# Second cross attention of a two layer decoder: projections at every other step, keys stacked piece by piece through DRAM

## The chip, the cores and the metric

The kernel runs on one core of one Trainium2 chip. The metric is the device time of one launch in microseconds; lower is better.

## The reference, cut to what matters

The kernel computes a two layer decoder on 16 sequences of 56 tokens with 128 channels. Each layer is self attention, cross attention over 1500 context rows, and a mixture of experts. The change touches the cross attention of the second layer only, with 16 heads of 8 channels:

```python
def _L1_xattn_ref(q, k, v, W_q, b_q, W_k, b_k, W_v, b_v, W_o, b_o):   # k = v = ctx, (16, 1500, 128)
    qh = _split_heads(q @ W_q.T + b_q, bs)
    kh = _split_heads(k @ W_k.T + b_k, bs)
    vh = _split_heads(v @ W_v.T + b_v, bs)
    scores = jnp.einsum('bhqd,bhkd->bhqk', qh, kh) / jnp.sqrt(jnp.float32(D_K))
    weight = jax.nn.softmax(scores, axis=-1)
    attn = jnp.einsum('bhqk,bhkd->bhqd', weight, vh)
    concat = attn.transpose(0, 2, 1, 3).reshape(bs, -1, D_MODEL)
    return concat @ W_o.T + b_o
```

## The kernel before

Every engine has a program of its own, written out by hand, and they meet in semaphores. In this stage TensorE, ScalarE, VectorE and SyncE walk the same loop: `for g in range(NC * B + LAG)`, with `b, c = g // 12, g % 12`. One loop over b has 12 steps c = 0 to 11. Three batches are in work at once.

For batch b + 1, TensorE computes in each step two of the 24 "maxima" products (L1085, 500 columns each); VectorE takes the row maximum of each (L1410). Unit u has piece u % 3 of the keys (500 of 1500 columns), so step 0 reads pieces 0 and 1 and step 1 begins with piece 2. For the batch four steps behind (n = g - LAG) it computes the scores of one chunk of 125 keys (L1105), ScalarE takes the exponential (L1329), GpSimd adds up the chunks (L1234), and in odd steps TensorE multiplies two chunks with the values (L1119). The sums (L1127) and their reciprocal and scaling on VectorE (L1456, L1457) are at step 7, VectorE's first addition (L1433) at step 6.

For batch b + 2 (in the 14 loops b = 0 to 13) the context is projected. `keys` on TensorE (L1044) makes a piece of 128 x 500 in PSUM bank 7; ScalarE writes its high part to `late_kH` (L1295; the tile prob_b), VectorE the low part to `late_kL` (L1404; the tile ctx_area). `values` (L1050) makes four chunks of the values in the same bank, and ScalarE takes them out (L1302). In `project`, TensorE waits before each piece until the one before has left bank 7:

```python
elif piece < 4:
    pe.wait_ge(m["khi"], 3 * b + piece)
    pe.wait_ge(m["klo"], 3 * b + piece)
else:
    pe.wait_ge(m["vev"], 3 * b + piece - 3)
```

Keys are projected at steps 2, 3, 4 and values at steps 6, 8, 10.

The score products want each quad of heads (32 rows) as a stack of 96 rows, high, high, low, in `late_k[b % 3]` (the tile HL). `stack` on SyncE (L1277) waits for all three pieces and copies by DMA from SBUF to SBUF: for each of 4 quads three transfers of 32 rows x 1500 values. TensorE's first maxima of the batch wait for all twelve (`m["stack"]`). After it SyncE loads the context of the next batch (L1266). Before the loop, a run-in of 12 steps computes the maxima of batch 0 and projects batch 1; stack(1) is then wanted at the first step of the loop.

Of the kernel before, what the change touches and what calls it, by code (L numbers as in the profile page):

```python
# [23 lines left out]
B, S, D = 16, 56, 128  # L24
# [9 lines left out]
S2 = 1500  # L34
KC = 125
NC = S2 // KC
KB = 500
# [18 lines left out]
ADDS = NC - 2  # L56
Q_BANKS, V_BANKS = (7, 3, 4, 5), (6, 7, 3)
# [14 lines left out]
def decoder_kernel(nc, t, out):  # L72
# [4 lines left out]
    with ctx:  # L77
# [159 lines left out]
        inv_kept = [nc.dram_tensor(f"inv_kept{g}", (128, SIZES[g]), fp32).ap() for g in range(2)]  # L237
        x_kept = nc.dram_tensor("x_kept", (128, NTOK), fp32).ap()
# [48 lines left out]
        names = ("wqrep qp qhi qlo q0set qset ones kmm khi klo stack vmm vev mxmm mx nmsplit nmtr nmcopy nmlow nmrow "  # L287
# [749 lines left out]
        def late_tensor(pe):  # L1037
# [32 lines left out]
            def maxima(b, u):  # L1070

                s, w = u // NKB, u % NKB
                if u == 0:
                    pe.wait_ge(m["stack"], 16 * 12 * (b + 1))
                    if b:
                        pe.wait_ge(m["qset"], b)
# [80 lines left out]
            def rest():  # L1157
# [30 lines left out]
                for g in range(NC * B + LAG):  # L1188
# [8 lines left out]
                    if b + 2 < B and c in (2, 3, 4):  # L1197
                        project(b + 2, c - 2)
                    if b + 2 < B and c in (6, 8, 10):
                        project(b + 2, c // 2)  # L1200
# [59 lines left out]
        def late_sync(sp):  # L1260
# [8 lines left out]
            def stack(b):  # L1269

                sp.wait_ge(m["khi"], 3 * (b + 1))
                sp.wait_ge(m["klo"], 3 * (b + 1))
                if b >= 3:
                    sp.wait_ge(m["sc"], 2 * NC * (b - 2))
                for j in range(4):
                    for r, half in enumerate((late_kH, late_kH, late_kL)):
                        sp.dma_start(late_k[b % 3][r * QUAD:(r + 1) * QUAD, j * S2:(j + 1) * S2].bitcast(fp32),  # L1277
                                     half[j * QUAD:(j + 1) * QUAD, :].bitcast(fp32)).then_inc(m["stack"], 16)
# [9 lines left out]
        def late_scalar(act):  # L1288
            m = la

            def keys(b, piece, bank):
                act.wait_ge(m["kmm"], 3 * b + piece + 1)
                if b and piece == 0:
                    act.wait_ge(m["stack"], 16 * 12 * b)
# [62 lines left out]
            def rest():  # L1357
# [18 lines left out]
                for g in range(NC * B + LAG):  # L1376
# [5 lines left out]
                    if b + 2 < B and c in (2, 3, 4):  # L1382
                        keys(b + 2, c - 2, 7)
                    if b + 2 < B and c in (6, 8, 10):
                        values(b + 2, c // 2 - 3, 7)
# [10 lines left out]
        def late_vector(dve, chain):  # L1396
            m = la

            def keys(b, piece, bank):
                dve.wait_ge(m["khi"], 3 * b + piece + 1)  # L1400
                if b and piece == 0:
                    dve.wait_ge(m["stack"], 16 * 12 * b)
# [61 lines left out]
            def rest():  # L1464
# [16 lines left out]
                for g in range(NC * B + LAG):  # L1481
# [9 lines left out]
                    if b + 2 < B and c in (2, 3, 4):  # L1491
                        keys(b + 2, c - 2, 7)
# [736 lines left out]
```

## Time and profile before

| | |
|---|---|
| median of 3 runs | 1412.35 us (1408.24 to 1413.59) |
| the profiled execution, its own time | 1414.38 us |
| its span | 1412.6 us |
| PE busy | 95% of the span |
| the loop described above | from 894 us to 1306 us |
| mean granted TensorE clock | 0.979 |

Busy shares are averages over unlike stages. A matmul's end is modelled, so that a row of two matmuls is longer than the time until the next one may start; what a step takes is read from start to start. "idle before <-releaser" gives the time the engine stood still and what released it. SPq is the queue of SyncE: its rows are the issuing of DMAs, not their data.

### The profile page before, as it was taken

What the parts mean: (1) busy time and instruction counts of PE and PEld (TensorE: products, weight loads), DVE (VectorE), ACT (ScalarE), POOL (GpSimd) and SP (SyncE); (2) the same over time, 40 slices, a digit from 0 to 9 for tenths busy, and PEclk for the clock granted to TensorE, in tenths of its full rate; (3) what the DMA queues carried; (4) which work ended last, traced back from release to release, by engine and by line L of the source; (5) the groups of instructions that cost most, each with busy time, mean ns of one, the idle gap of its engine ahead of it and who ended that gap; (6) DMA issues with size and microseconds to landing.
All of it is one profiled execution on the core that took longest, in us unless ns stands there. A gap on an engine that the chain in (4) does not pass through costs nothing.

```text
span 1412.6 us, 25408 instructions
## 1 busy us (share of the span) xinstructions
PE 1337.2 (95%) x9220; PEld 1037.2 (73%) x9220; DVE 1051.9 (74%) x2127; ACT 863.9 (61%) x1849; POOL 735.0 (52%) x416
## 2 busy tenths in 40 slices
PE   7889999999999999999998987899999999999998
PEld 4548888888888888888875854566666666665687
DVE  6558778888778777888854577777778778785787
ACT  4537667666666666676632554466666666665675
POOL 5136443334444444433151374187887887884463
PEclk9999999999999999999998899899999999998999
DMA  3132222211122222221150130644645536440131
GB/s 86 60 94 52 57 58 58 53 39 41 47 56 58 52 57 58 57 58 28 44 160 2 59 77 25 142 119 103 140 111 120 144 88 147 97 96 2 59 109 42
DMA packets 71803, 104.39 MB, mean 74 GB/s; under 512 B 14670, under 2 KB 54934, under 8 KB 71550
## 3 DMA queue, kind: packets, MB, share of 16 engines
q1 hardware_dynamic: 60062, 91.39, 25.9%
q10 hardware_dynamic: 11616, 11.38, 2.9%
q8 instruction: 73, 1.20, 0.4%
q14 instruction: 52, 0.43, 0.1%
HBM read 63.65 MB, written 2.11 MB: 47 GB/s over the span
## 4 chain that ended last, share of the span: by engine, by line
PE 81%; DVE 9%; DMA 3%; ACT 3%; SPq 2%; issue 1%; ACTq 0%; POOL 0%; DVEq 0%; POOLq 0%
PE PS L702 10%; PE PS L716 6%; PE PS L690 5%; PE PS L1105 5%; PE PS L1085 5%; PE PS L1119 5%; PE PS L691 5%; PE PS L692 5%; PE PS L718 5%; PE PS L717 5%; PE PS L1044 3%; SPq L1277 2%; PE PS L1792 2%; PE PS L745 2%; PE PS L1794 2%; PE PS L1793 2%
## 5 line engine op out<-in xcount | busy, mean ns | idle before, releaser
L1234 POOL TENSOR_TENSOR QO_area<-QO_area,prob_a 125x896 f32<-125x896 f32 x150 | 315.2, 2101 | 100.2 <-DVE QO_area L1433 80.3
L868 ACT ACTIVATE HL<-PS 125x512 fp32r<-125x512 f32 (+1 forms) x384 | 206.6, 539 | 178.1 <-PE PS L702 161.3
L960 DVE TENSOR_TENSOR HL<-PS,HL 125x512 fp32r<-125x512 f32 (+1 forms) x384 | 238.1, 622 | 74.5 <-ACT HL L868 53.4
L1410 DVE TENSOR_REDUCE QO_area<-PS 112x1 f32<-112x500 f32 x384 | 237.4, 670 | 44.3 <-PE PS L1085 44.1
L1329 ACT ACTIVATE prob_a<-PS 125x448 f32<-125x448 f32 x384 | 187.6, 540 | 122.6 <-PE PS L1105 117.3
L775 POOL TENSOR_TENSOR HL<-ctx_area,ones 125x512 fp32r<-125x512 f32 (+1 forms) x64 | 93.0, 1453 | 245.4 <-PE PS L718 191.5
L1085 PE MATMUL PS<-HL 96*112 96x500 f32 x384 | 157.8, 480 | 16.9 <-DVE QO_area L1410 12.1
L716 PE MATMUL PS<-HL 125*128 125x512 f32 (+1 forms) x384 | 155.7, 405 | 2.2 <-DVE HL L960 1.7
L690 PE MATMUL PS<-HL 128*128 128x500 f32 x336 | 152.8, 455 | 4.3 <-DVE HL L930 3.9
L878 ACT ACTIVATE prob_a<-prob_a,neg_max 128x500 f32<-128x500 f32 x192 | 135.5, 707 | 25.3 <-DVE neg_max L952 24.0
L718 PE MATMUL PS<-HL 125*128 125x512 f32 (+1 forms) x384 | 140.4, 366 | 0.0
L717 PE MATMUL PS<-HL 125*128 125x512 f32 (+1 forms) x384 | 140.1, 365 | 0.0
L1105 PEld LDWEIGHTS PS<-HL 98*125 98x125 f32 x768 | 118.6, 190 | 27.8 <-ACT prob_a L1329 7.8
L1105 PE MATMUL PS<-HL 98*125 98x256 f32 x768 | 133.1, 293 | 2.8 <-ACT prob_a L1329 2.8
L691 PE MATMUL PS<-HL 128*128 128x500 f32 x336 | 130.9, 389 | 0.0
L692 PE MATMUL PS<-HL 128*128 128x500 f32 x336 | 130.6, 389 | 0.0
L702 PEld LDWEIGHTS PS<-ident,prob_a 128*125 128x125 f32 x768 | 113.4, 186 | 17.3 <-ACT prob_a L878 0.8
L1085 PEld LDWEIGHTS PS<-HL 96*112 96x112 f32 x384 | 60.8, 179 | 82.2 <-DVE QO_area L1410 56.7
L778 POOL TENSOR_TENSOR HL<-ctx_area,HL 125x512 fp32r<-125x512 f32 (+1 forms) x64 | 116.6, 1822 | 5.0
L702 PE MATMUL PS<-ident,prob_a 128*125 128x128 f32 x768 | 115.3, 272 | 0.4 <-ACT prob_a L878 0.4
L878 ACT ACTIVATE prob_b<-prob_b,neg_max 128x500 f32<-128x500 f32 x144 | 101.8, 707 | 0.0
L775 POOL TENSOR_TENSOR HL<-QO_area,ones 128x896 fp32r<-128x896 f32 x15 | 25.2, 1680 | 142.6 <-PE PS L692 129.0
(260 smaller groups left out, 2727.0 us busy)
## 6 DMA issues: line engine op xcount, KB each, us to landing
HL<-prob_b SPq DMA_DIRECT2D x128, 187.5 KB, 3.9
ctx_area<-in_ctx_T SPq DMA_DIRECT2D x16, 750.0 KB, 13.1
ctx_area<-in_ctx SPq DMA_DIRECT2D x16, 750.0 KB
HL<-ctx_area SPq DMA_DIRECT2D x64, 187.5 KB, 3.8
inv_area<-in_ctx_T SPq DMA_DIRECT2D x8, 750.0 KB, 4.1
prob_a<-in_ctx_T SPq DMA_DIRECT2D x8, 750.0 KB, 4.4
inv_area<-inv_kept ACTq DMA_DIRECT2D x16, 256.0 KB, 3.4
ctx_area<-in_L_ffn_W SPq DMA_DIRECT2D x16, 256.0 KB, 3.2
```

Source lines behind the costliest of these rows:

```text
L690: nc.tensor.matmul(dst, qH[b % 2][:, rows], kH[b % 2][:, cols], start=True, stop=False)
L702: mm = nc.tensor.transpose(PS[0:KC, 2 + k % 3, j * 128:(j + 1) * 128], tile_prob(GA * g + j)[:, k * KC:(k + 1) * KC], ident[:, :])
L716: nc.tensor.matmul(dst, v_hi, p_hi, start=k == 0, stop=False)
L717: nc.tensor.matmul(dst, v_lo, p_hi, start=False, stop=False)
L718: nc.tensor.matmul(dst, v_hi, p_lo, start=False, stop=k == NC - 1).then_inc(m["pv"], 1)
L868: nc.scalar.activation(pH[k % 3][0:KC, 0:width(g)], PS[0:KC, 2 + k % 3, 0:width(g)], ACT.Copy)\
L878: nc.scalar.activation(p, p, ACT.Exp, bias=neg_max[:, s:s + 1], accum_out=part_sum[:, s, j:j + 1]).then_inc(m["exp"], 1)
L960: nc.vector.tensor_tensor(pL[k % 3][0:KC, 0:width(g)], PS[0:KC, 2 + k % 3, 0:width(g)], pH[k % 3][0:KC, 0:width(g)].bitcast(fp32), ALU.sub ...
L1085: nc.tensor.matmul(PS[0:2 * S, w, 0:KB], late_q[b % 3][0:3 * QUAD, s * 2 * S:(s + 1) * 2 * S], late_k[b % 3][0:3 * QUAD, at:at + KB], star ...
L1105: mm = nc.tensor.matmul(PS[0:KC, 3 + half, a * SCOLS:(a + 1) * SCOLS], late_k[b % 3][:, j * S2 + c * KC:j * S2 + (c + 1) * KC], late_q[b % ...
L1234: nc.gpsimd.tensor_tensor(acc, acc, late_p[n % LATE_P], ALU.add).then_inc(m["padd"], 1)
L1410: nc.vector.tensor_reduce(late_part[b % 2][:, u // NKB, u % NKB:u % NKB + 1], PS[0:2 * S, u % NKB, 0:KB], AX, ALU.max).then_inc(m["mx"], 1)
```

## The change

The projections move to steps 2, 4, 6 (keys) and 8, 10, 11 (values). VectorE takes the low part of a key piece one step later (steps 3, 5, 7). `stack` works piece by piece: when a piece is ready, two transfers write its high and low part (128 x 500 each) to a DRAM scratch `keys_kept`, SyncE waits for both, and three transfers read it back, each to 32 rows and all four quads. There is a semaphore for each piece, and TensorE's first three maxima units each wait for their own.

```diff
--- before.py
+++ after.py
@@ -54,6 +54,7 @@
 LATE_P = 5
 SUM_STEP = (3, 7)
 ADDS = NC - 2
+PROJECTED = (2, 4, 6, 8, 10, 11)
 Q_BANKS, V_BANKS = (7, 3, 4, 5), (6, 7, 3)
 LAG = 4
 SCOLS = 256
@@ -235,6 +236,7 @@
         slot_kept = nc.dram_tensor("slot_kept", (E * B, S), fp32).ap()
         gates_kept = [nc.dram_tensor(f"gates_kept{l}", (E * B, S), fp32).ap() for l in range(2)]
         inv_kept = [nc.dram_tensor(f"inv_kept{g}", (128, SIZES[g]), fp32).ap() for g in range(2)]
+        keys_kept = [[nc.dram_tensor(f"keys_kept{i}{h}", (128, S2), fp32).ap() for h in range(2)] for i in range(2)]
         x_kept = nc.dram_tensor("x_kept", (128, NTOK), fp32).ap()
         vo_kept = nc.dram_tensor("vo_kept", (128, NH * 128), fp32).ap()
         vo_first = [x.rearrange("p (h c) -> p h c", h=NH // 2) for x in free[0:2]]
@@ -284,7 +286,7 @@
         ld_k = [sem("ld_k0")]
         ld_late = [sem(f"ld_late{i}") for i in range(2)]
 
-        names = ("wqrep qp qhi qlo q0set qset ones kmm khi klo stack vmm vev mxmm mx nmsplit nmtr nmcopy nmlow nmrow "
+        names = ("wqrep qp qhi qlo q0set qset ones kmm khi klo split stack0 stack1 stack2 vmm vev mxmm mx nmsplit nmtr nmcopy nmlow nmrow "
                  "sc exp pv first padd sum norm wo out").split()
         la = {n: sem(f"late_{n}") for n in names}
         ld_v = sem("ld_v")
@@ -1070,10 +1072,10 @@
             def maxima(b, u):
 
                 s, w = u // NKB, u % NKB
-                if u == 0:
-                    pe.wait_ge(m["stack"], 16 * 12 * (b + 1))
-                    if b:
-                        pe.wait_ge(m["qset"], b)
+                if u < NKB:
+                    pe.wait_ge(m[f"stack{w}"], 16 * 3 * (b + 1))
+                if u == 0 and b:
+                    pe.wait_ge(m["qset"], b)
                 if b == 0:
                     if u < NKB:
                         pe.wait_ge(m["qlo"], u + 1)
@@ -1194,10 +1196,8 @@
                     if 0 <= n:
                         scores(n // NC, n % NC, 0)
                         scores(n // NC, n % NC, 1)
-                    if b + 2 < B and c in (2, 3, 4):
-                        project(b + 2, c - 2)
-                    if b + 2 < B and c in (6, 8, 10):
-                        project(b + 2, c // 2)
+                    if b + 2 < B and c in PROJECTED:
+                        project(b + 2, PROJECTED.index(c))
                     if c == 0 and 0 <= b < B:
                         turn_maxima(b)
                     if n % 2:
@@ -1268,14 +1268,22 @@
 
             def stack(b):
 
-                sp.wait_ge(m["khi"], 3 * (b + 1))
-                sp.wait_ge(m["klo"], 3 * (b + 1))
-                if b >= 3:
-                    sp.wait_ge(m["sc"], 2 * NC * (b - 2))
-                for j in range(4):
-                    for r, half in enumerate((late_kH, late_kH, late_kL)):
-                        sp.dma_start(late_k[b % 3][r * QUAD:(r + 1) * QUAD, j * S2:(j + 1) * S2].bitcast(fp32),
-                                     half[j * QUAD:(j + 1) * QUAD, :].bitcast(fp32)).then_inc(m["stack"], 16)
+                for w in range(NKB):
+                    sp.wait_ge(m["khi"], 3 * b + w + 1)
+                    sp.wait_ge(m["klo"], 3 * b + w + 1)
+                    if b >= 3 and w == 0:
+                        sp.wait_ge(m["sc"], 2 * NC * (b - 2))
+                    if b >= 2:
+                        sp.wait_ge(m[f"stack{w}"], 16 * 3 * (b - 1))
+                    c = slice(w * KB, (w + 1) * KB)
+                    for h, half in enumerate((late_kH, late_kL)):
+                        sp.dma_start(keys_kept[b % 2][h][:, c], half[:, c].bitcast(fp32)).then_inc(m["split"], 16)
+                    sp.wait_ge(m["split"], 16 * 2 * (NKB * b + w + 1))
+                    for r, h in enumerate((0, 0, 1)):
+                        dst = late_k[b % 3][r * QUAD:(r + 1) * QUAD, :].rearrange("p (j n) -> p j n", j=4)
+                        sp.dma_start(dst[:, :, c].bitcast(fp32),
+                                     keys_kept[b % 2][h][:, c].rearrange("(j p) n -> p j n", j=4))\
+                            .then_inc(m[f"stack{w}"], 16)
 
             load(0)
             sp.wait_ge(x_ready, 3)
@@ -1290,8 +1298,8 @@
 
             def keys(b, piece, bank):
                 act.wait_ge(m["kmm"], 3 * b + piece + 1)
-                if b and piece == 0:
-                    act.wait_ge(m["stack"], 16 * 12 * b)
+                if b:
+                    act.wait_ge(m[f"stack{piece}"], 16 * 3 * b)
                 nc.scalar.activation(late_kH[:, piece * KB:(piece + 1) * KB], PS[:, bank, 0:KB], ACT.Identity,
                                      bias=xa_bias[:, 1:2]).then_inc(m["khi"], 1)
 
@@ -1379,10 +1387,10 @@
                     if 0 <= n:
                         exps(n // NC, n % NC, 0)
                         exps(n // NC, n % NC, 1)
-                    if b + 2 < B and c in (2, 3, 4):
-                        keys(b + 2, c - 2, 7)
-                    if b + 2 < B and c in (6, 8, 10):
-                        values(b + 2, c // 2 - 3, 7)
+                    if b + 2 < B and c in PROJECTED[0:3]:
+                        keys(b + 2, PROJECTED.index(c), 7)
+                    if b + 2 < B and c in PROJECTED[3:6]:
+                        values(b + 2, PROJECTED.index(c) - 3, 7)
                     if b + 2 < B and c == 5:
                         queries(b + 2)
                     if c == 0 and 0 <= b < B:
@@ -1398,8 +1406,8 @@
 
             def keys(b, piece, bank):
                 dve.wait_ge(m["khi"], 3 * b + piece + 1)
-                if b and piece == 0:
-                    dve.wait_ge(m["stack"], 16 * 12 * b)
+                if b:
+                    dve.wait_ge(m[f"stack{piece}"], 16 * 3 * b)
                 c = slice(piece * KB, (piece + 1) * KB)
                 nc.vector.scalar_tensor_tensor(late_kL[:, c], PS[:, bank, 0:KB], xa_bias[:, 1:2],
                                                late_kH[:, c].bitcast(fp32), ALU.add, ALU.subtract)\
@@ -1488,8 +1496,8 @@
                         maxima(b + 1, 2 * c + 1)
                     if c == 1 and 0 <= b < B:
                         low_maxima(b)
-                    if b + 2 < B and c in (2, 3, 4):
-                        keys(b + 2, c - 2, 7)
+                    if b + 2 < B and c - 1 in PROJECTED[0:3]:
+                        keys(b + 2, PROJECTED.index(c - 1), 7)
                     if n >= 0 and n % NC == 2:
                         first_add(n // NC)
                     if n > NC * (B - 1) + 1:
@@ -1878,7 +1886,8 @@
                     .then_inc(ld_w[par], 16)
 
             sp.wait_ge(la["vmm"], 3 * B)
-            sp.wait_ge(la["stack"], 16 * 12 * B)
+            for w in range(NKB):
+                sp.wait_ge(la[f"stack{w}"], 16 * 3 * B)
             for e in range(E):
                 load(e, e % 2)
```

## Rows read from the trace of the kernel before

**Rows 1.** One loop; columns: stretch, busy times, PE clock, DMA share, GB/s.

```profile
core 0: us, PE busy (x) PEld busy (x) DVE busy (x) ACT busy (x) POOL busy (x), PEclk, DMA share, GB/s
...
1035.00:1062.00 27.00, 25.82 (x216) 17.87 (x215) 20.67 (x34) 18.49 (x38) 22.51 (x12) 1.00 0.48 116
```

**Rows 2.** Waits between 930 and 1250 us: us in total, times, longest.

```profile
PE PS L1044 <- DVE ctx_area L1404: 8.5, 12, 0.7
...
PEld PS L1085 <- DMA HL<-ctx_area: 6.1, 12, 1.6
```

**Rows 3.** Timeline from step 10 of a loop to step 4 of the next.

```profile
1046.56 0.71 PE L1085 MATMUL PS<-HL 96*112 96x500 f32 x2
...
1047.58 1.04 PE L1050 MATMUL PS<-proj_w,prob_a 128*125 128x128 f32 x8
...
1048.38 0.70 PE L1085 MATMUL PS<-HL 96*112 96x500 f32 x2
...
1050.37 0.71 PE L1085 MATMUL PS<-HL 96*112 96x500 f32 x2
...
1051.42 0.69 PE L1085 MATMUL PS<-HL 96*112 96x500 f32 x2
...
1053.71 0.73 PE L1085 MATMUL PS<-HL 96*112 96x500 f32 x2
...
1055.20 1.02 PE L1085 MATMUL PS<-HL 96*112 96x500 f32 x2
...
1056.51 0.74 DVE L1404 SCALAR_TENSOR_TENSOR ctx_area<-PS,xa_bias,prob_b 128x500 fp32r<-128x500 f32 x1 [1.02 <-ACT prob_b L1295]
...
1057.39 1.08 PE L1044 MATMUL PS<-inv_area,proj_w 128*128 128x500 f32 x2 [0.70 <-DVE ctx_area L1404]
...
1059.30 0.71 PE L1085 MATMUL PS<-HL 96*112 96x500 f32 x2
```

**Rows 4.** SyncE's queue in one loop.

```profile
1037.49 1.14 SPq L1277 DMA_DIRECT2D HL<-prob_b  x2
...
1062.88 1.14 SPq L1277 DMA_DIRECT2D HL<-prob_b  x2
```

**Rows 5.** Columns as in rows 1: the stack, then a write to DRAM.

```profile
1039.00:1047.00 8.00, 7.51 (x77) 5.58 (x76) 7.23 (x11) 5.05 (x11) 5.80 (x3) 1.00 0.99 215
67.10:69.80 2.70, 2.70 (x6) 1.39 (x5) 0.00 (x0) 0.88 (x4) 0.00 (x0) 0.65 0.97 388
```

**Rows 6.** SyncE's queue around that write (two transfers, 1.05 MB).

```profile
66.27 0.82 SPq L643 DMA_DIRECT2D vo_kept<-ctx_area  x2
70.21 0.33 SPq L815 DMA_DIRECT2D ctx_area<-in_ctx_T  x1
```

**Rows 7.** TensorE around the DMA wait at the start of loop 1.

```profile
918.44 0.96 PE L1119 MATMUL PS<-prob_a,QO_area 125*32 125x224 f32 x16
921.09 0.71 PE L1085 MATMUL PS<-HL 96*112 96x500 f32 x2 [1.68 <-DMA HL<-ctx_area]
```

**Rows 8.** Columns as in rows 1: after the DMA waits at 894 and 921.

```profile
898.00:902.00 4.00, 3.20 (x5) 1.12 (x4) 2.33 (x4) 0.68 (x1) 0.00 (x0) 0.50 0.00 1
...
922.00:924.00 2.00, 2.00 (x14) 1.63 (x16) 2.00 (x5) 1.11 (x4) 1.86 (x2) 0.58 0.12 49
924.00:926.00 2.00, 2.00 (x19) 0.89 (x19) 0.21 (x2) 0.97 (x2) 1.86 (x2) 0.57 0.02 4
```

**Rows 9.** SyncE's queue: where the stacks of loops 0 and 1 begin.

```profile
907.60 1.14 SPq L1277 DMA_DIRECT2D HL<-prob_b  x2
...
934.78 1.14 SPq L1277 DMA_DIRECT2D HL<-prob_b  x2
```

**Rows 10.** Run-in: VectorE's first low part, TensorE's first steps of loop 0.

```profile
876.93 0.74 DVE L1404 SCALAR_TENSOR_TENSOR ctx_area<-PS,xa_bias,prob_b 128x500 fp32r<-128x500 f32 x1
...
894.24 0.68 PE L1085 MATMUL PS<-HL 96*112 96x500 f32 x2 [1.44 <-DMA HL<-ctx_area]
...
894.78 0.55 PE L1085 MATMUL PS<-HL 96*112 96x500 f32 x1
```

## The prediction

> **What bounds the kernel now.** I read the busy times first. In this stage TensorE is busy for 25.8 of 27 us, VectorE for 20.7 and GpSimd for 22.5, at full clock, with the DMA engines half used [rows 1]. So TensorE is nearest to a bound, but a row of two matmuls overlaps what follows, and its busy share does not say that it never stands. The reader should next take the waits: bank 7 makes it stand for a key piece's eviction (8.5 us over 12 loops), and the stack's DMA for 6.1 us over 12 loops, once for each loop [rows 2]. Then the timeline, from first maxima matmul to first maxima matmul (1000 us left off here): step 10, with a values projection, takes 46.56 to 48.38 = 1.82 us, step 11 (with two chunks of products) in 48.38 to 50.37 = 1.99, step 0 in 1.05, step 1 (products) in 2.29, step 2 (keys) in 1.49, but step 3, with keys and products, takes 55.20 to 59.30 = 4.10. In it the second key matmul starts at 57.39, after VectorE's low part (56.51 plus 0.74) has ended [rows 3]. Last, SyncE's queue: the stack begins 25.39 us after the one before it, which is the length of a loop, and its twelve transfers, started at 37.49, let TensorE go on at 50.37, 12.88 us later [rows 3, 4]. From there to the next stack are 12.51 us. Those two terms are the whole loop, so the loop is closed by a chain through the DMA: keys, stack, maxima, keys. It is this chain, more than TensorE's work, that the change rearranges.
>
> **Step 3 and step 11.** The number of matmuls, evictions and reductions stays the same. Steps 2 and 3 together are 5.59 us now. After the change step 2 keeps one projection (1.82, as step 10) and step 3 has products alone (2.0, as step 11): 3.82 together, 1.77 less. Steps 4 and 6 keep a projection each, and steps 8 and 10 too. Step 11 gains one: from 47.58 to 48.38 [rows 3], 0.80 us. Waits at the new places: the second key piece, at step 4, wants the low part made in step 3; step 3's reductions and low part end 0.45 + 1.25 + 0.74 = 2.44 us after step 3 begins, which is 0.44 into step 4, and the projection there comes 1.0 us into the step, as in step 10 (47.58). No wait. The piece at step 11 wants the eviction of step 10, with a step between. No wait. A loop would be 25.39 - 1.77 + 0.80 = 24.4 us by TensorE, 14 loops 13.6 us less.
>
> **VectorE.** Two low parts move into steps 5 and 7, where its first addition, the reciprocal and the scaling already crowd it. It loses the waits for ScalarE in steps 3 and 4 and so comes to step 5 earlier, by about the 1.5 us that it waits there now; 2 x 0.74 = 1.48 us more work [rows 3] lies there. I count 0; without that cover it is 1.5 us for each loop.
>
> **The stack.** This is the large term. L is the time from the first low part (in step 3, no longer step 4) until piece 2 has landed. TensorE reads pieces 0 and 1 in step 0 and piece 2 first in step 1. How much L is allowed? From step 4 to step 0 are 59.30 to 50.37 + 25.39 = 75.76, 16.46 us; plus 0.80 in step 11 and 1.05 for step 0 make 18.3; the low part ends 0.44 into step 4, so 17.9 us. From step 1 back to the low part are 2.29 + 1.82 + 2.44 = 6.55 us. The loop is therefore the larger of 24.4 and L + 6.55.
>
> What is L? The trace before has no round trip of this size, so I build it from two neighbours. A write of 1.05 MB to DRAM by two transfers: the issue at 66.27, all the data between 67.10 and 69.80 (2.70 us x 388 GB/s is the whole of it), SyncE going on at 70.21 [rows 5, 6]. So 0.83 us until data flow, 388 GB/s, 0.4 us until the waiter goes on. The two writes of a piece (0.512 MB): 0.83 + 1.32 + 0.4 = 2.5 us. The reads, 0.768 MB, go to 32 rows each, as the stack's transfers do now, and those run at 215 GB/s with the DMA engines 99% busy [rows 5]: 3.57 us. I take that rate, since the destination has the same shape; by the whole stack (2.304 MB in 12.88 us less 1.2 for start and end) it is 198 GB/s, 3.88 us. SyncE waits for the writes before it issues the reads, and the next piece's writes stand in the queue behind those reads, so one piece after another costs 1.32 + 0.4 + 0.83 + 3.57 = 6.1 us; the low parts come every 3.8 us and do not hold it up. L = 0.83 + 3 x 6.12 + 0.4 = 19.6, or 20.5 at 198 GB/s. I take 19.9, nearer to the rate that the row gives itself. If the reads ran at the 388 GB/s of the write, issuing would set the pace (2.5 us for the writes, then three issues at 0.57, as 1.14 for two [rows 4]: some 4.3 us a piece), and L would be about 14.5. If each wait cost 0.9 us more, as the stack's 12.88 us suggest when 215 GB/s is its rate, L would be 22.6.
>
> So the loop is 19.9 + 6.55 = 26.45 us, 1.06 more than now, with TensorE standing 2.0 us for piece 2 in each loop: 14 x 1.06 = 14.8 us. The context load, behind the stack in SyncE's queue, has more than a loop of slack.
>
> A rule of the Trainium skill bears on this rate. In "SBUF — State Buffer", section "Door 1: The DMA port swizzle", rows 0 to 31 of SBUF reach only 8 of its 16 DMA ports, with an asymptote of about 218 GB/s. The stack's 215 GB/s agree. By that page's figure an estimate of L is 19.4, and the sum would be 7 us smaller than with 19.9.
>
> **The clock.** TensorE's DMA wait of 1.68 us at the start of loop 1 [rows 7] was followed by a granted clock of 0.58 and 0.57 in the two stretches after 922, which is some 3.4 us at the lower level, 1.2 GHz. The wait of 1.44 us at 894 [rows 10] was followed by the lower level too, and for longer [rows 8]. The weight loads' DMA waits of up to 1.6 us between 930 and 1250 [rows 2] were not, as loops there stayed at full clock [rows 1]. What it costs: from 921.09 to the next stack at 934.78 are 13.69 us, against 12.51 in the undisturbed loop [rows 4, 7, 9]: 1.2 us. With 2.0 us of standing I am just above the wait that brought it, so I count it in half of the loops: 7 x 1.2 = 8.4 us; none is 0, all are 16.8.
>
> **The run-in.** The first low part of batch 1 ends at 877.67 (876.93 plus 0.74), and TensorE reads piece 2 at 894.78 [rows 10]. 877.67 + 19.9 = 897.6: 2.8 us later. The stack of batch 0 was issued some 50 us before it is read and stays hidden.
>
> **Sum.** 14.8 + 8.4 + 2.8 = 26 us on the profiled execution's 1414.4 us, 1440.4. That execution lies 2.0 above the median of the runs, so I predict 1438 us.
>
> **The rivals.** 0.5% (7 us) is about what a measurement of this kernel can tell from no change.
>
> Not slower: the stack lands in time. It decides at L = 17.9, that is, if a piece takes 5.6 us instead of 6.1 to 6.4. For it: nothing in the rows shows reads from DRAM to 32 rows, and the present transfers have both ends in 32 rows, so the source may be what halves them. Against it: the destination is unchanged. Then 13.6 us less, and the run-in's DMA wait of 1.4 us goes: 1412.35 - 15 = 1397. A second rule of the Trainium skill gives this result: "DMA: Bandwidth & Descriptors", the table of the two cost components, prices a DMA at 2.0 us plus its bytes at 436 GB/s. An estimate by it is 3.2 us for the writes and 3.8 for the reads, with the next writes issued while the reads run: L about 16.5. The 12.88 us for the stack's 2.3 MB show that this rate does not hold for transfers to 32 rows.
>
> No difference: L between 18.3 and 19.2, where the late piece eats what step 3 gives back: 1405 to 1419, say 1412.
>
> Slower still: the clock falls in each loop and L is 20.5: 14 x (1.66 + 1.2) + 3.4 = 43, so 1455. With longer waits, L = 22.6, it is over 1480.
>
> VectorE becomes the bound: its 1.5 us are not covered. With the stack in time: 14 x (1.5 - 0.97) = +7.4, so 1420. Against it, VectorE has 6 us to spare in each loop [rows 1].
>
> The change doesn't do what it says: if the piece at step 4 or 6 waits for the low part all the same, the 1.77 us are not got. By the times above there is a margin of about 0.6 us.
>
> **How the numbers follow.** The stack is late and the loop longer (the forecast, with more or less of the clock's fall): 0.50, by itself 1419 to 1459. Stack in time: 0.29. No difference: 0.15. VectorE as the bound: 0.03. L over 22: 0.03. Faster 0.29, same 0.16 (with a little of the edge of the forecast), slower 0.55. The range must take in the case in time, at 1397, and the one with the clock falling in each loop, at 1455 and some us for a slower read: 1397 to 1459, with little left out at both ends.
>
> **What would show it.** Right: TensorE's wait on the DMA at the second maxima row of each loop (step 1), about 2 us; two transfers to keys_kept and three from it, 6 us from piece to piece; loops of 26 to 28 us; the granted clock under 1.00 in some of the stretches between 930 and 1250; the wait of the key matmul for the low part gone. Wrong: stretches of three reads at well over 215 GB/s, or no DMA wait at step 1, with loops of 24.4 us. Also wrong would be a wait of the key matmuls in step 4 or 6, or of the maxima for VectorE around steps 8 and 9.

## The result, and the profile after

The changed kernel takes 1501.95 us (median, 1497.97 to 1504.15), the kernel before 1410.3 us in the same series; the ratio is 1.0645 [1.061, 1.0679]. The prediction had the direction and the place right (1438 us, slower), but the time lies 43 us above the top of its range. The profiled execution took 1502.2 us, with a span of 1500.4 us and a mean granted clock of 0.948.

First the waits of the kernel after between 930 and 1300 us (us in total, times, longest), which answer to [rows 2]:

```profile
PEld PS L1087 <- DMA HL<-keys_kept: 65.1, 12, 6.9
PE PS L1087 <- DMA HL<-keys_kept: 61.8, 12, 6.6
```

There is still one wait for the stack in each loop, but 5.2 us long instead of 0.5. The wait of the key matmul for the low part (8.5 us in [rows 2]) is gone, as forecast. The same view for SyncE's own queue shows where the stack's time goes:

```profile
SPq L1275 <- PE PS L1107: 136.9, 12, 11.9
SPq L1284 <- DMA keys_kept<-ctx_area: 134.0, 34, 5.9
```

The second row is the round trips: before its reads, SyncE stands 3.9 us on average for the writes. One loop of that queue, which answers to [rows 4] (start, length of issuing; L1280 writes to DRAM, L1284 reads back):

```profile
1003.22 0.34 SPq L1280 DMA_DIRECT2D keys_kept<-prob_b  x1
...
1007.58 1.27 SPq L1284 DMA_DIRECT2D HL<-keys_kept  x3
1008.96 0.36 SPq L1280 DMA_DIRECT2D keys_kept<-prob_b  x1
...
1014.23 1.27 SPq L1284 DMA_DIRECT2D HL<-keys_kept  x3
1015.61 0.37 SPq L1280 DMA_DIRECT2D keys_kept<-prob_b  x1
...
1021.12 1.27 SPq L1284 DMA_DIRECT2D HL<-keys_kept  x3
1022.44 0.43 SPq L1266 DMA_DIRECT2D prob_a<-in_ctx_T  x1
1034.63 0.34 SPq L1280 DMA_DIRECT2D keys_kept<-prob_b  x1
...
1037.35 1.27 SPq L1284 DMA_DIRECT2D HL<-keys_kept  x3
```

From piece to piece are 6.65 and 6.89 us, and the next stack begins 31.41 us after this one (25.39 before). TensorE in the same loop:

```profile
1021.11 0.26 PE L1095 MATMUL PS<-ident,QO_area 112*8 112x112 f32 x1
1026.80 1.18 PE L1087 MATMUL PS<-HL 96*112 96x500 f32 x2 [5.43 <-DMA HL<-keys_kept]
...
1030.38 0.70 PE L1087 MATMUL PS<-HL 96*112 96x500 f32 x2
...
1031.84 1.00 PE L1087 MATMUL PS<-HL 96*112 96x500 f32 x2
...
1034.13 0.71 PE L1087 MATMUL PS<-HL 96*112 96x500 f32 x2
```

TensorE stands at step 1, where the forecast put it, and goes on 5.68 us after the last reads were issued. Steps 2 and 3 are 30.38 to 34.13 = 3.75 us, against 5.59 before and 3.82 forecast. Step 1 itself takes 3.58 us, against 2.29 in [rows 3]: it runs at half clock. The stretches show it, with columns as in [rows 1]. The first three are of the DMA: most of the first writes, then the packets from piece to piece (three reads and the next piece's two writes), twice:

```profile
1003.90:1005.20 1.30, 1.30 (x7) 0.74 (x6) 0.80 (x3) 1.20 (x3) 1.30 (x1) 1.00 0.94 351
1008.51:1013.70 5.19, 4.50 (x47) 3.27 (x45) 5.16 (x8) 3.30 (x7) 4.13 (x2) 1.00 0.94 247
1015.15:1020.60 5.45, 5.45 (x54) 4.38 (x47) 2.88 (x6) 3.36 (x7) 5.07 (x3) 1.00 0.95 238
...
1020.00:1024.00 4.00, 1.37 (x11) 0.90 (x7) 1.26 (x2) 1.10 (x3) 3.71 (x3) 0.93 0.57 135
1024.00:1028.00 4.00, 1.20 (x4) 0.99 (x5) 0.40 (x1) 0.00 (x0) 0.94 (x1) 0.50 0.96 273
1028.00:1032.00 4.00, 4.00 (x29) 2.42 (x28) 2.14 (x5) 1.62 (x4) 2.10 (x1) 0.71 0.00 1
1032.00:1036.00 4.00, 4.00 (x32) 2.50 (x30) 3.33 (x6) 2.87 (x6) 3.44 (x2) 1.00 0.13 50
```

The clock falls to 1.2 GHz during the stand, and between 1028 and 1032 it goes back to 2.4 GHz. This happens in every loop of the trace. The whole loop beside that of [rows 1]: less TensorE work in 27 us, at a lower clock, while the DMA engines are not full.

```profile
1008.00:1035.00 27.00, 20.88 (x176) 14.81 (x175) 16.22 (x27) 12.65 (x26) 19.19 (x10) 0.87 0.59 153
```

Cut into the forecast's own terms (from SyncE's rows and TensorE's resumptions, as above, over the 15 stacks of the stage):

| | forecast | measured, mean |
|---|---|---|
| first writes to first reads | 2.5 | 3.3 (2.72 in eleven, 4.36 to 5.12 in four) |
| from reads to reads, twice | 2 x 6.12 | 2 x 6.94 |
| last reads to TensorE going on | 4.8 | 6.05 (5.56 to 7.05) |
| L, the sum | 19.9 taken | 23.2 |
| way back, step 1 to first low part | 6.55, plus 0.6 of clock | 8.6 (7.8 to 9.3, full loops) |
| loop | 27.05 | 31.88 |

In loop 0 TensorE goes on from its wait for piece 2 at 902.34. The forecast had 897.6, and the kernel before reads that piece at 894.78: 7.6 us later, not 2.8.

### The profile page after: what moved, and what is told of

Same layout as the page of the kernel before. It is cut to its first block, busy times and chain, and to the rows that moved or that the text cites. A ratio compares the mean times of both kernels' runs of the same rounds, so it can differ in the third digit from the quotient of the medians.

```text
span 1500.4 us, 25594 instructions
## 1 busy us (share of the span) xinstructions
PE 1357.7 (90%) x9220; PEld 1054.1 (70%) x9220; DVE 1050.4 (70%) x2127; ACT 861.5 (57%) x1849; POOL 735.0 (49%) x416
## 4 chain that ended last, share of the span: by engine, by line
PE 65%; DMA 19%; DVE 7%; SPq 4%; ACT 2%; issue 2%; POOL 1%; ACTq 0%; POOLq 0%; DVEq 0%
DMA keys_kept<-ctx_area 13%; PE PS L704 9%; PE PS L718 6%; PE PS L692 5%; DMA HL<-keys_kept 5%; PE PS L720 5%; PE PS L693 5%; PE PS L719 5%; PE PS L694 5%; SPq L1284 3%; PE PS L1087 3%; PE PS L1107 2%; PE PS L1121 2%; PE PS L1800 2%; PE PS L747 2%
## 5 line engine op out<-in xcount | busy, mean ns | idle before, releaser
L1087 PE MATMUL PS<-HL 96*112 96x500 f32 x384 | 169.8, 516 | 92.9 <-DMA HL<-keys_kept 78.0
L1087 PEld LDWEIGHTS PS<-HL 96*112 96x112 f32 x384 | 64.0, 193 | 168.8 <-DMA HL<-keys_kept 82.4
L1107 PEld LDWEIGHTS PS<-HL 98*125 98x125 f32 x768 | 127.4, 203 | 28.2 <-ACT prob_a L1337 7.1
L1107 PE MATMUL PS<-HL 98*125 98x256 f32 x768 | 136.6, 302 | 2.9 <-ACT prob_a L1337 2.9
L946 DVE CUSTOM_DVE_ANT_0 prob_a<-PS,proj_w,head_scale 128x500 f32<-128x500 f32 x128 | 93.5, 731 | 6.3 <-PE PS L694 2.0
```

The costliest lines, as they stand in the source:

```text
L1087: nc.tensor.matmul(PS[0:2 * S, w, 0:KB], late_q[b % 3][0:3 * QUAD, s * 2 * S:(s + 1) * 2 * S], late_k[b % 3][0:3 * QUAD, at:at + KB], star ...
L1107: mm = nc.tensor.matmul(PS[0:KC, 3 + half, a * SCOLS:(a + 1) * SCOLS], late_k[b % 3][:, j * S2 + c * KC:j * S2 + (c + 1) * KC], late_q[b % ...
```

## The experiments

The median of the kernel before, run beside each, was 1412.7 to 1413.7 us.

**e1: maxima piece by piece.** The 24 maxima of a batch go through piece 0 for all eight groups of heads, then piece 1, then piece 2, which is so wanted at step 8 instead of step 1.

```diff
-                s, w = u // NKB, u % NKB
-                if u < NKB:
+                s, w = (u // NKB, u % NKB) if b == 0 else (u % 8, u // 8)
+                if s == 0:
                     pe.wait_ge(m[f"stack{w}"], 16 * 3 * (b + 1))
```

> The changed kernel, with one thing different: from batch 1 on, the 24 maxima units of a batch go piece by piece (units 0 to 7 read piece 0, 8 to 15 piece 1, 16 to 23 piece 2) instead of 0, 1, 2, 0, 1, 2. Piece 2 is then first read in step 8, not in step 1; all transfers stay. Theory (the loop is closed by the chain from the low part through the DRAM round trips to piece 2 in step 1): the wait goes, the clock stays at 1.00, a loop takes 24.4 us, the kernel about 1397 us (1390 to 1405). Rival (the traffic itself, 4.5 MB a loop, or the low parts in steps 5 and 7 slow the engines): it stays above 1430.

Measured: 1399.1 us (1394.38 to 1401.23), ratio 0.9889 [0.9854, 0.9924]. TensorE has no wait for a stack between 930 and 1300. The transfers are as slow as in the changed kernel:

```profile
1022.91 1.27 SPq L1287 DMA_DIRECT2D HL<-keys_kept  x3
...
1029.71 2.39 SPq L1287 DMA_DIRECT2D HL<-keys_kept  x3
...
1036.87 1.27 SPq L1287 DMA_DIRECT2D HL<-keys_kept  x3
```

And a stretch at full clock:

```profile
1035.00:1062.00 27.00, 26.31 (x230) 19.18 (x233) 21.64 (x36) 18.95 (x41) 23.43 (x12) 1.00 0.61 162
```

So all of the loss goes, and a gain is left (1399.1 us against 1413.7 before, beside it), by nothing but a later use of piece 2: 103 us between this run and the changed kernel, with the DMA's load as it was. That load does cost a little. In five loops TensorE now stands for the small transfer that brings the maxima into HL:

```profile
PE PS L1110 <- DMA HL<-QO_area: 4.2, 5, 1.3
```

The loops are 25.0 us on average; by TensorE alone the forecast had 24.4.

**e2: the new places alone.** `stack` is that of the kernel before, twelve transfers from SBUF to SBUF after the third piece, with one semaphore.

```diff
-                if u < NKB:
-                    pe.wait_ge(m[f"stack{w}"], 16 * 3 * (b + 1))
+                if u == 0:
+                    pe.wait_ge(m["stack"], 16 * 12 * (b + 1))
```

> The new places of the projections and low parts, with the old stack: twelve SBUF to SBUF transfers after the last low part. That comes in step 7 now, 15.4 us after the step 0 before it, and the stack takes 12.9 us. Theory (a chain through the DMA in this form too): a loop of 28.3 us, and 1 to 1.5 us more where the clock falls, so 1453 to 1475 us. Rival (the DRAM round trips alone are at fault, the spaced places are a gain): 1397 to 1412 us.

Measured: 1479.71 us (1478.23 to 1486.73), ratio 1.0473 [1.0434, 1.0513]. The stack's rows:

```profile
1031.08 1.14 SPq L1277 DMA_DIRECT2D HL<-prob_b  x2
...
1061.80 1.14 SPq L1277 DMA_DIRECT2D HL<-prob_b  x2
```

And TensorE's resumption:

```profile
1043.94 1.18 PE L1087 MATMUL PS<-HL 96*112 96x500 f32 x2 [3.84 <-DMA HL<-ctx_area]
```

The transfers keep their 12.86 us (12.88 before). The way back is 61.80 - 43.94 = 17.86 us instead of 12.51, because the third low part now comes in step 7, and the clock falls too. The forecast had 1 us a loop saved for TensorE by the spacing. The chain pays 3 us for it at full clock (from step 0 to the end of the last low part are 15.5 us in e6's trace, against 12.51): with this stack the spacing is a loss by itself.

**e3: the DRAM stack alone**, with the projections at their old places.

```diff
-PROJECTED = (2, 4, 6, 8, 10, 11)
+PROJECTED = (2, 3, 4, 6, 8, 10)
...
-                    if b + 2 < B and c - 1 in PROJECTED[0:3]:
+                    if b + 2 < B and c in PROJECTED[0:3]:
```

> The piecewise stack through DRAM, with the projections and low parts at their old places (keys at steps 2, 3, 4 with the low part in the same step). Piece 0 starts about a step earlier. Theory: 23.6 us from low part to landing as in the changed kernel, 5.8 us back from step 1 to the low part, 1.3 for the clock: a loop of 30.7 us, the kernel 1487 us (1475 to 1500). Rival (the old places hide the new stack): 1412 us or less.

Measured: 1481.03 us (1472.09 to 1481.79), ratio 1.0458 [1.0415, 1.0501]. L is 22.4 us with first writes always at 2.7, and TensorE's DMA wait is 2.9 us on average:

```profile
PE PS L1087 <- DMA HL<-keys_kept: 34.3, 12, 4.0
```

Each half of the change costs 66 to 67 us alone, and both together 92: they are two ways of lengthening one chain, not two separate losses. The clock fell in 13 of the 14 loops after the first, most with stands of only 2.0 to 3.0 us. In this stretch TensorE goes on at 1045.60, after 2.10 us:

```profile
1045.00:1049.00 4.00, 3.40 (x22) 2.13 (x22) 1.43 (x3) 0.98 (x2) 3.71 (x3) 0.52 0.38 147
```

**e4 and e5: small matmuls in the wait.** TensorE multiplies into bank 2 ahead of the wait for piece 2, to see what the clock costs.

```diff
+                if u == 2 and b >= 2:
+                    pe.wait_ge(m["mx"], NKB * 8 * b + u - 2)
+                    for i in range(FILL):                  # 40 in e4, 22 in e5
+                        nc.tensor.matmul(PS[:, 2, 0:64], ones[:, :], ident[:, 0:64], start=True, stop=True)
                 if u < NKB:
                     pe.wait_ge(m[f"stack{w}"], 16 * 3 * (b + 1))
```

> The changed kernel with 40 small matmuls (64 columns, results not used) on TensorE ahead of the wait for piece 2, from batch 2 on; they take some 4.5 of the 5.5 us in which TensorE stands there. It prices the clock by itself. Theory (the lower clock after the wait costs 1.3 us on the way back to the low part in each loop): about 18 to 25 us less than the changed kernel, 1477 to 1484 us. Rival (the fall costs nothing, as the loop is set by the DMA): 1502 us.

Measured: 1517.4 us (1514.07 to 1530.32), ratio 1.0749. A miss: each matmul became two instructions, and the 80 took 9.05 us, longer than the wait itself.

```profile
1021.52 9.05 PE L1079 MATMUL PS<-ident,ones 128*128 128x64 f32 x80
1030.39 0.68 PE L1092 MATMUL PS<-HL 96*112 96x500 f32 x2
```

> As the kernel with 40 small matmuls ahead of the wait for piece 2, with 22 of them. The 40 took 9.05 us (two instructions each), more than the wait they were to fill; 22 take 5.0 us of the 5.5. Theory (the clock's fall is a price of its own): the clock stays at 1.00, the way from step 1 back to the first low part is 6.3 us instead of 7.8, and the kernel takes about 1480 us (1474 to 1486), 22 less than the changed kernel. Rival (the fall is free, because the DMA sets the loop): 1502 us.

Measured: 1493.86 us (1486.21 to 1502.91), ratio 1.0574 [1.0508, 1.0639]; 8 us below the changed kernel, not 22, and by the two intervals not clear of it.

```profile
1046.53 5.03 PE L1079 MATMUL PS<-ident,ones 128*128 128x64 f32 x44
1053.18 0.71 PE L1092 MATMUL PS<-HL 96*112 96x500 f32 x2 [1.61 <-DMA HL<-keys_kept]
```

The first maxima row takes 0.71 us here and 1.18 in the changed kernel: the clock is up. From 1053.18 the next stack begins at 1059.44, 6.26 us later, against the 6.55 that the forecast had for full clock and the 8.6 measured after. So the fall costs 2.3 us in a loop. But the filler does not hold the clock everywhere. In five of the 14 loops after the first it falls all the same, as here, where TensorE goes on at 1020.74, and the ways back there are 7.8 to 9.2 us:

```profile
1020.00:1024.00 4.00, 3.26 (x22) 1.88 (x22) 1.43 (x3) 0.98 (x2) 0.88 (x1) 0.64 0.38 149
```

Nine loops of 2.3 us are 21 us. About half is lost again in SyncE's rows: the first writes take 3.2 to 5.2 us in ten of 15 stacks (mean 3.8, 3.3 after), from the second reads to the third are 7.5 us (6.95 after) and from the first to the second 6.7 (6.9), together 0.8 us more a loop, or 11 us. That leaves 10; the loops of the two traces differ by 0.70 us, which is also 10. Some loops also stand for piece 1 in step 0. What goes with the slower transfers is shown under "Slow first writes" below.

**e6: no round trip.** From batch 1 on, the reads take what was written a batch before, so that SyncE need not wait (the maxima and scores are then of other keys). Same transfers, same bytes, same queue.

```diff
-                    sp.wait_ge(m["split"], 16 * 2 * (NKB * b + w + 1))
+                    sp.wait_ge(m["split"], 16 * 2 * (NKB * (b - 1) + w + 1))   # b >= 1
...
-                                     keys_kept[b % 2][h][:, c]
+                                     keys_kept[max(b - 1, 0) % 2][h][:, c]
```

> The changed kernel, but from batch 1 on SyncE reads back the keys that were written for the batch before, so that it does not wait for the writes just issued: the same transfers and bytes in the same order, without the round trip (the scores are those of other keys). Theory (each piece pays its write's completion and the read's start): a piece costs the 5.3 us of its data alone, L falls from 23.6 to about 17.7 us, and TensorE hardly waits: 1397 to 1412 us. Rival (the bytes in one queue are all of it): above 1450 us.

Measured: 1393.27 us (1392.44 to 1397.15), ratio 0.9865 [0.9818, 0.9912]. Writes and reads are now issued together:

```profile
1022.20 0.34 SPq L1280 DMA_DIRECT2D keys_kept<-prob_b  x1
1022.58 0.43 SPq L1280 DMA_DIRECT2D keys_kept<-ctx_area  x1
1023.06 1.51 SPq L1287 DMA_DIRECT2D HL<-keys_kept  x3
...
1046.70 0.34 SPq L1280 DMA_DIRECT2D keys_kept<-prob_b  x1
```

The loop is 24.50 us; the forecast for TensorE alone was 24.4. Without the order "write, wait, read" in series, the same bytes land in time. They count only inside that order, as e7 shows.

**e7: one read less.** From batch 3 on the second high copy is not read back.

```diff
-                    for r, h in enumerate((0, 0, 1)):
+                    for r, h in ((0, 0), (2, 1)) if b >= 3 else ((0, 0), (1, 0), (2, 1)):
```

> The changed kernel without the second copy of the high part from batch 3 on: two reads a piece instead of three (the scores use stale rows there). Round trips are the same in number. If the rate into 32 rows (215 GB/s) is the price, each piece is 1.2 us shorter, L 3.6 us, and the loop some 26.5 to 28 us: 1435 to 1455 us. If the fixed times of the round trips are, and bytes are not: above 1485 us.

Measured: 1425.24 us (1419.03 to 1431.62), ratio 1.0084 [1.0057, 1.0111]. From reads to reads are 5.6 us (12 stacks), 1.36 less; the forecast's price of a read was 1.19, so a read's bytes were priced nearly right. The run also shows where the wait begins. Where the first writes take 2.7 us, L is 18.4 to 19.3 and the loop 24.5 to 25.6 us; where they take 4.6 to 5.0, L is 20.3 to 21.1 and the loops are 28.1 to 29.8 us, with ways back of 7.8 to 9.1 instead of 6.3. The allowed L of the forecast was 17.9. With L at 20.3 to 21.1, which is a stand of 2.1 to 2.9 us, the clock fell in three of four loops; the fourth, with L at 20.4, kept it and took 26.7 us.

**e8: the stack from SBUF to SBUF in two parts**, pieces 0 and 1 together and then piece 2, at the new places.

```diff
...
+                for i, (first, last) in enumerate(((0, 2), (2, 3))):
+                    sp.wait_ge(m["khi"], 3 * b + last)
+                    sp.wait_ge(m["klo"], 3 * b + last)
...
+                    for j in range(4):
+                        for r, half in enumerate((late_kH, late_kH, late_kL)):
+                            sp.dma_start(late_k[b % 3][r * QUAD:(r + 1) * QUAD, j * S2 + first * KB:j * S2 + last * KB]
+                                         .bitcast(fp32),
+                                         half[j * QUAD:(j + 1) * QUAD, first * KB:last * KB].bitcast(fp32))\
+                                .then_inc(m[f"stack{i}"], 16)
```

> The new places of the projections and low parts, with the stack copied from SBUF to SBUF as before the change, in two parts: the first 1000 columns after the low part in step 5 (12 transfers of 125 KB), the last 500 after that in step 7 (12 of 62.5 KB). Theory (only lateness at steps 0 and 1 counts): the second part lands 8.4 us after its low part, 10 us are allowed, so there is no wait: a loop of 24.4 us, about 1397 us. Rival (24 issues at 0.6 to 1 us are too many for SyncE's queue): the second part is late by 2 us or more, and the kernel at 1430 or above.

Measured: 1471.68 us (1470.97 to 1479.0), ratio 1.0426 [1.0372, 1.0479].

```profile
1025.01 1.14 SPq L1280 DMA_DIRECT2D HL<-prob_b  x2
...
1040.76 0.59 SPq L1280 DMA_DIRECT2D HL<-ctx_area  x1
```

Then TensorE:

```profile
1042.88 0.71 PE L1089 MATMUL PS<-HL 96*112 96x500 f32 x2 [3.45 <-DMA HL<-ctx_area]
```

24 transfers need 16.3 us to be issued, 0.68 each, without a gap between the two parts, and TensorE goes on 1.5 us after the last. Meanwhile the DMA engines are busy for 58%:

```profile
1025.00:1042.00 17.00, 13.74 (x125) 10.17 (x123) 12.25 (x19) 10.07 (x22) 13.68 (x7) 1.00 0.58 133
```

Issuing is the limit here, the rival's case.

**e9: one of the reads to 128 rows.** From batch 3 on the second high copy goes to an idle area of 128 rows instead of 32 rows of the stack.

```diff
+                        if b >= 3 and r == 1:
+                            sp.dma_start(ctx_area[:, S2 + w * KB:S2 + (w + 1) * KB], keys_kept[b % 2][h][:, c])\
+                                .then_inc(m[f"stack{w}"], 16)
+                            continue
```

> The changed kernel, in which from batch 3 on the second of a piece's three reads goes to 128 rows of an idle area instead of 32 (the same 250 KB; the scores use stale rows). Without that read the kernel took 1425 us, with it in 32 rows 1502. If what slows the reads is that the destination has only 32 rows (215 GB/s against the 388 of a transfer over 128 rows: 1.19 us against 0.66), the wide read costs 55% of what the narrow one does: 1425 + 0.55 x 77 = about 1467 us (1455 to 1478). If it is bytes and reads in number: 1495 to 1505 us.

Measured: 1495.94 us (1493.39 to 1500.86), ratio 1.0583 [1.0553, 1.0613]; reads to reads 6.85 us (13 stacks), 6.94 after. A third of the read bytes going to four times the rows saves 0.1 us a piece at most; the expectation had half a microsecond. My choice of the stack's 215 GB/s "since the destination has the same shape" gave nearly the right rate (reads alone ran at 198, see e13) for a reason that this run does not bear out.

**e10 and e12: what the places are worth** once piece 2 is not wanted early. e10 is e1 with the old places (the edit of e3); e12 is e1 again, beside it.

> As e1_piece_order, with projections and low parts at their old places. Nobody waits for the stack in either, so the difference is the places alone. By the forecast's terms (1.77 us got in step 3, 0.80 given back in step 11): 13.6 us more than e1_piece_order, about 1412 us. Rival (the places are worth nothing): 1399 us.

> e1_piece_order once more, beside the two above on one chip, to compare them: 1399 us within 4.

Measured: e10 1408.74 us (1403.86 to 1411.38), ratio 0.9964 [0.9941, 0.9986]; e12 1398.07 us (1396.78 to 1398.98), ratio 0.9886 [0.9865, 0.9907]. The spaced projections are worth 10.7 us. In e10 the wait for the low part is back, as in [rows 2] but for the lines' numbers; the second row, of e12, is a wait that e10 does not have:

```profile
PE PS L1049 <- DVE ctx_area L1415: 8.5, 12, 0.7
...
PE PS L1110 <- DMA HL<-QO_area: 3.7, 4, 1.4
```

**e11: maxima piece by piece with the SBUF stack of e8.** The edits of e1 and e8 together.

> The new places, the stack from SBUF to SBUF in two parts as in e8_direct_two_parts, and the maxima in the order of the pieces from batch 1 on, so that the late second part is first read in step 8. Theory (e8 was late only because 24 issues take 16 us in SyncE's queue): no wait is left, 1395 to 1402 us, the same as e1_piece_order, with 3 MB a loop moved instead of 4.5. Rival: above 1412 us.

Measured: 1393.52 us (1393.16 to 1395.74), ratio 0.9854 [0.983, 0.9878], the fastest that computes everything: 20 us below the kernel before and 108 below the changed one. The DRAM scratch is not needed for it: without its 1.5 MB a loop of more traffic the wait for HL<-QO_area is gone too, and the time is 4.6 us below that of e12.

```profile
1008.00:1035.00 27.00, 26.30 (x240) 18.58 (x240) 22.39 (x37) 17.94 (x38) 23.16 (x11) 1.00 0.54 132
```

**e13: no context load behind the stack.** From batch 4 on keys and values are made of the contexts of batches 2 and 3.

```diff
                 stack(b)
-                if b + 2 < B:
+                if b + 2 < 4:
                     load(b + 2)
```

> The changed kernel, but the context of batches 4 to 15 is not loaded; their keys and values come from the contexts of batches 2 and 3. Every other instruction stays. In the changed kernel the context load (0.77 MB) is issued right behind the last three reads of a stack, and TensorE goes on 6.05 us after those reads are issued (mean of 15 loops), not 4.8 as forecast. Theory: the last reads share the DMA engines with that load. Then 4.8 to 5.1 us here, the loop 1.0 to 1.3 us shorter, 1483 us (1479 to 1489). Rival: the end of a read is late by itself; 6.05 us stay and the time is 1500 (1495 to 1504). The first writes should keep their 2.7 us in most loops and 4.4 to 5.1 in some; if the long ones go, the load had to do with them, and it is some 0.5 us a loop more.

Measured: 1495.07 us (1489.14 to 1496.19), ratio 1.0589 [1.0564, 1.0614]. From the last reads to TensorE going on are 5.38 to 5.71 us (mean 5.55 of the 14 loops after the first), where the changed kernel has 5.98 without its first stack. Both theories miss, each by half: 0.4 us come from the load that shares the DMA engines, and 0.75 above the forecast's 4.8 stay. The trace shows where, since these reads now run alone; this is one of them, issued at 1076.11, from its first to its last packet, and TensorE goes on at 1081.60:

```profile
1077.00:1080.90 3.90, 0.78 (x6) 0.46 (x5) 1.26 (x2) 1.10 (x3) 3.73 (x2) 0.85 0.87 198
```

On average the data flow after 0.94 us (0.83 in the forecast), for 3.87 us (3.57), and TensorE goes on 0.75 us after the last packet (0.4). The kernel's 7 us are 0.5 us in 14 loops, and the loops of the two traces differ by 0.44. The first writes still take 4.6 to 5.2 us in four of 15 stacks, so the load has nothing to do with those.

**Slow first writes.** The first writes of a stack, with nothing else of SyncE's queue beside them, take 2.72 us in most stacks and 3.2 to 5.3 in others. The DMA view tells them apart. Between 1034.5 and 1037.4, with 2.72 us, it has one queue; between 1098.0 and 1103.3, with 5.12 us, there is a second one (packets, MB, share of 16 engines):

```profile
q1 hardware_dynamic: 288, 0.51, 46.7%
...
q1 hardware_dynamic: 288, 0.51, 25.7%
q8 instruction: 1, 0.02, 2.2%
```

This is one packet of 16 KB on a queue that the profile calls "instruction". In seven traces (after, e3, e4, e5, e7, e9, e13) there are 105 such stacks. In 27 such a packet runs while the first writes' data flow, and these 27 take 3.2 to 5.3 us; the other 78 have none and take 2.7. The later pieces go the same way: in the changed kernel nine of 30 have one and take 7.34 us on average, the others 6.76. In e5, whose matmuls are more instructions, 25 of 45 have one, against 13 in the changed kernel. No run changed these packets alone, so that they cause the delay is argued from this agreement, not tested.

## Why the prediction was right in kind and wrong in size

**The bound.** Right. The loop is closed by the chain of keys, stack and maxima. e1 and e6 each take the chain away by other means (a later use, no serial wait) and both come out at TensorE's loop, 24.5 to 25.0 us.

**Step 3 and step 11.** Right: 3.75 us for 3.82, and e10 against e12 gives 10.7 us for 13.6; e12's 3.7 us for HL<-QO_area are the greater part of the difference.

**VectorE.** Nearly right: there is no wait of the projections for low parts, and with the chain out of the way (e1, e11) TensorE is busy 26.3 of 27 us. But a sign that the prediction named as wrong is there. At step 8 the maxima wait for VectorE, 0.69 us a time; the kernel before has the same wait with 0.48 (6.2 us in 13 times), so the term is 0.2 us a loop and not 0:

```profile
PE PS L1087 <- DVE QO_area L1418: 7.6, 11, 0.7
```

**The stack, L.** This is the step that failed. The method (writes, wait, reads, in series) stands, but every part of it was priced too short. The parts sum to 19.6 in the forecast and 23.2 measured; it took 19.9:

- A piece takes 6.94 us instead of 6.12. Two thirds of that lie in the bytes: 1.32 + 3.57 = 4.89 us were forecast for 1.28 MB, and the packets of the 30 pieces run for 5.43 us on average. Reads alone ran at 198 GB/s (e13), where the forecast took 215, and writes alone at 351, where it took 388.
- The rest lies around the bytes. "0.83 us until data flow, 388 GB/s, 0.4 us until the waiter goes on" came from one large write [rows 5, 6]. Here these times are 0.94 and 0.56 us, 1.50 together instead of 1.23.
- The first writes take 3.3 us instead of 2.5: 0.2 in every stack, and the rest from the four slow ones.
- The last reads take 6.05 us instead of 4.8: 0.75 by themselves (e13), 0.4 from the context load and the rest from the first stack. That load was said to have "more than a loop of slack". It has, but it takes time from the reads ahead of it.

The prediction named a case near to this, "each wait cost 0.9 us more", L = 22.6, and worked it out as over 1480. It gave it 0.03, though the stack's own 12.88 us had suggested just that. With the measured L of 23.2, the forecast's 6.55 and its 1.2 us of clock in each loop, its own sum comes to 1496 us, 6 below the result: the mechanism was right, and the sizes were wrong. The Trainium skill's "DMA: Bandwidth & Descriptors", its table of the two cost components, would have given an estimate of 16.5 for L; the trace shows 23.2. The Trainium skill's "SBUF — State Buffer", section "Door 1: The DMA port swizzle", gives about 218 GB/s for rows 0 to 31. The reads alone, to rows 0 to 95 by 32 each, ran at 198 (e13), so that figure is near; but e9 shows no effect of the number of rows, so no run here shows that the ports set this rate.

**The clock.** Second failed term. "I count it in half of the loops" at 1.2 us: it falls in all, after stands of 3.6 to 6.6 us instead of the 2.0 forecast, and costs 2.3 us (way back 8.6 after, 6.26 at full clock in e5). In part it follows from L, since the stands are longer. But e3 shows that half of the loops was too few by itself: with most stands at 2.0 to 3.0 us, the clock fell in 13 of 14.

**The run-in.** Sized wrong by the same term: 7.6 us for 2.8. Of the 4.8 us between them, 3.2 are L (23.1 us for 19.9), and 1.6 come from the first low part, which VectorE ends at 879.20 instead of 877.67.

**The sum.** The transposition at the end of step 0 (L1095) marks the loops of the kernel after:

```profile
L1095 PE MATMUL PS<-ident,QO_area x3: 259/259/260, 895.8 to 959.0; 112*8 112x112 f32 x3
```

The first stands at 895.8, the 15th at 1341.5: 31.83 us a loop. Before, they stand at 894.75 and 1254.77: 25.72 a loop, since three of the 14 loops take 26.6 to 27.4; my 25.39 was that of an undisturbed one, 0.33 too short. So the loops cost 14 x (31.83 - 25.72) = 85.7 us of the 87.8 between the two profiled executions. The forecast had 14 x (27.05 - 25.39) + 2.8 = 26. A loop is 4.8 us longer than forecast: 3.3 of it in L and 1.45 in the way back (8.6 for 7.15).

**The rivals.** The stack in time, 1397, is the time that e1 and e6 measure without the chain (1399 and 1393); so the worth of the case was right, and its condition (5.6 us a piece) is missed by 1.3. In e7, at 5.6 us a piece, the loops with short first writes are in fact at 24.5 to 25.6 us: the edge lies where the forecast put it.

**Open.** Whether the packets of the instruction queue cause the slow first writes, as their agreement suggests; it is neither the context load (e13) nor the width of the reads (e9, 4.6 to 5.0 in four). Also what sets the rate of the reads, 198 GB/s: the number of rows that they go to does not (e9).

## What to carry to other kernels

When a loop is closed by a chain through the DMA, a change that eases the compute engine but spreads the chain out or adds serial steps to it can lose, as both halves of this one did. Work out the chain's length first. A small error in the price of a transfer, in its rate or in the time around it, counts as often as the chain has transfers in series (here three pieces, 0.8 us each). A later use is cheaper than a faster transfer: reordering the maxima by piece was worth 103 us here, with each transfer as slow as before. And where a stand also brings the clock down, an error in one term is paid twice.

## What the runs showed of the hardware that was not expected

- A write of 0.512 MB to DRAM, from issue to the waiter going on, takes 2.72 us alone in the queue and 5.6 behind three reads issued 1.4 us ahead of it. In 27 of 105 stacks of seven traces the first one took 3.2 to 5.3 us, just those in which a 16 KB packet of the "instruction" queue ran meanwhile.
- Reads from DRAM of 2000 bytes a row ran alone at 198 GB/s (e13), such writes alone at 351, and both together at 236 (5.43 us for 1.28 MB, mean of 30 pieces), with the DMA engines 94 to 95% busy in the two stretches shown. One of three reads going to 128 rows instead of 32 changed a piece by 0.1 us at most (e9).
- A stand of 3.6 to 6.6 us in each loop went with the lower clock in each, though TensorE was busy almost without a gap between the stands. Stands of 2.0 to 4.0 us did so in 13 of 14 loops (e3).
- A transfer from SBUF to SBUF of 32 rows costs 0.59 us or more of issuing in SyncE's queue (0.68 on average in e8), one from or to DRAM mostly 0.32 to 0.43.
